# The running minimum of the scores: seeded from eviction to eviction, with ln 255 added on ScalarE

## What is computed

```python
q = _fq_sym(q, axis=-1)                       # rounded to 127 steps, per row
k = _fq_sym(k, axis=-1)
v = _fq_sym(v, axis=2)
attn = jnp.einsum('bhqd,bhkd->bhqk', q, k)    # 16 heads x 4096 queries x 8192 keys
attn = jax.nn.softmax(attn.astype(jnp.float32), axis=-1)
attn = _fq_unsigned(attn, axis=-1)            # round(255 * attn / max(attn)), per row
out = jnp.einsum('bhqk,bhkd->bhqd', attn, v)
```

## Time and profile before

| | us |
|---|---|
| runs shown | 6421.83, 7106.4, 6457.51 |
| their median | 6457.51 |
| the profiled execution | 6431.73 |
| its span, first to last instruction | 6430.2 |
| VectorE busy | 5619.6 (87%) |
| ScalarE busy | 4772.4 (74%) |
| GpSimd busy | 4588.0 (71%) |
| TensorE busy | 4487.4 (70%) |

### The profile page before, as it was taken

One profiled execution on the slowest core, in us unless ns is written; L12 is line 12 of the kernel. 1 busy time (PEld: TensorE's weight loads), 2 busy tenths in 40 slices (PEclk: granted clock), 3 DMA queues, 4 the chain that ended last, 5 costly groups with the idle time before them and its releaser, 6 DMA issues. The chain is left out here.

```text
span 6430.2 us, 141911 instructions
## 1 busy us (share of the span) xinstructions
PE 4487.4 (70%) x48939; PEld 2136.5 (33%) x49654; DVE 5619.6 (87%) x7587; ACT 4772.4 (74%) x6550; POOL 4588.0 (71%) x3259
## 2 busy tenths in 40 slices
PE   7556666666666666666666666666666646769999
PEld 3322222222222222222222222232222233455555
DVE  8799999999999999999999999999999936872222
ACT  5479998998999899989999988989989933331111
POOL 4578888888898888888888888888888823420000
PEclk9899999999999999999999999999999978979999
DMA  4267777777777777777777777777777730010000
GB/s 127 76 123 139 140 142 146 139 144 142 142 143 141 143 139 141 142 140 140 142 142 145 139 138 139 147 140 141 145 141 141 138 87 0 0 36 4 7 8 9
DMA packets 2231984, 735.80 MB, mean 114 GB/s; under 512 B 2175781, under 2 KB 2209416, under 8 KB 2225577
## 3 DMA queue, kind: packets, MB, share of 16 engines
q1 hardware_dynamic: 2196265, 576.08, 44.0%
q0 software_dynamic: 35456, 157.33, 13.8%
HBM read 168.97 MB, written 27.26 MB: 31 GB/s over the span
## 5 line engine op out<-in xcount | busy, mean ns | idle before, releaser
L914 DVE TENSOR_SCALAR_CACHE_REDUCE scores<-ring,step 128x2048 f32<-128x2048 f32 (+2 forms) x2560 | 4780.0, 1918 | 50.5 <-PE ring L841 38.1
L973 ACT ACTIVATE n_op<-scores,bias 128x2048 uint8<-128x2048 f32 x2048 | 4076.2, 1997 | 284.6 <-DVE m_rest L921 284.5
L789 POOL CAST nT<-pairs 128x2048 f16<-128x2048 uint8 x2048 | 3791.1, 1890 | 510.9 <-DMA pairs<-n_op 491.4
L841 PE MATMUL ring<-x_all,q_op 128*128 128x512 bf16 x7746 | 2147.6, 385 | 702.2 <-DVE scores L914 630.5
L841 PEld LDWEIGHTS ring<-x_all,q_op 128*128 128x128 bf16 x8192 | 682.2, 98 | 1854.1 <-DVE scores L914 1180.6
L838 PE MATMUL ring<-x_all,q_op 128*128 128x512 bf16 x1793 | 571.9, 389 | 775.2 <-DVE scores L914 744.1
L853 PE MATMUL pO<-nT,v_op 128*32 128x128 f16 x32768 | 659.0, 223 | 141.0 <-ACT att_g L991 109.0
L853 PEld LDWEIGHTS pO<-nT,v_op 128*32 128x32 f16 x32768 | 481.6, 98 | 590.2 <-issue 512.2
L838 PEld LDWEIGHTS ring<-x_all,q_op 128*128 128x128 bf16 x2048 | 116.7, 97 | 997.8 <-DVE scores L914 979.4
L973 ACT ACTIVATION_READ_ACCUMULATOR n_op<-scores,bias 128x1 f32 x2048 | 396.1, 193 | 0.0
L1752 DVE TENSOR_TENSOR h_up<-h_gate,pUp 128x512 f32<-128x512 f32 x112 | 76.9, 687 | 298.8 <-ACT h_gate L1741 298.8
(11 more groups left out here) (202 smaller groups left out, 3616.1 us busy)
## 6 DMA issues: line engine op xcount, KB each, us to landing
x_all<-keys_transposed POOLq DMA_DIRECT2D x128, 768.0 KB, 8.5
v_st<-value_integers POOLq DMA_DIRECT2D x128, 256.0 KB, 3.5
pairs<-n_op SPq DMA_TRANSPOSE x2048, 2.8
keys_transposed<-kT_s POOLq DMA_DIRECT2D x32, 384.0 KB, 3.3
cT<-in_ctx_T SPq DMA_DIRECT2D x32, 256.0 KB, 2.6
x_all<-in_x SPq DMA_DIRECT2D x2, 4096.0 KB, 16.2
q_op<-queries_transposed POOLq DMA_DIRECT2D x384, 16.0 KB, 8.4
value_integers<-v_int SPq DMA_DIRECT2D x1, 4096.0 KB, 13.0
```

What stands on the lines that cost most here:

```text
L789: nc.gpsimd.tensor_copy(nT[par][:, j * EK:(j + 1) * EK, :].rearrange("p (a c) b -> p a c b", c=2), src).then_inc(s_un, 1)
L841: mm = nc.tensor.matmul(slot(t, j)[:, n * BANK:(n + 1) * BANK], q_op[b][:, t * P:(t + 1) * P], k_op[b][:, at + n * BANK:at + (n + 1) * BAN ...
L914: nc.vector.tensor_scalar(score[t % 2][:, at:at + width * BANK], slot(t, j)[:, 0:width * BANK], step[b][:, t:t + 1], None, ALU.mult, ALU.m ...
L973: nc.scalar.activation(n_op[par][:, j * EW:(j + 1) * EW], score[par][:, j * EW:(j + 1) * EW], ACT.Exp, bias=bias[par][:], scale=-1.0, accu ...
```

## The change

The combination of minima (`make_bias`) and its place in VectorE's order go. From the second piece of a unit on, an eviction waits for the one in front of it and takes that one's minimum, column j - 1 of `m_part`, as a second per-row operand, so that column j holds the minimum over pieces 0 to j. ScalarE waits for the unit's last eviction, adds the constant ln 255 from a new tile to its column with an Identity activation of 128 x 1, and waits for that before the first exponential.

```diff
-        DVE_STEPS = "D0 BIAS D1 D2 D3 INV D4".split()
+        DVE_STEPS = "D0 D1 D2 D3 INV D4".split()
...
+        ln_255 = sb("ln_255", [P, 1], F32, xs)
...
+                nc.gpsimd.memset(ln_255[:], LN255).then_inc(s_init, 1)
...
                     dve.wait_ge(s_m, scored(u, j))
+                    least = None
+                    if j > 0:
+                        dve.wait_ge(s_mu, scored(u, j - 1))
+                        least = m_part[t % 2][:, j - 1:j]
                     nc.vector.tensor_scalar(score[t % 2][:, at:at + width * BANK], slot(t, j)[:, 0:width * BANK],
-                                            step[b][:, t:t + 1], None, ALU.mult, ALU.min,
+                                            step[b][:, t:t + 1], least, ALU.mult, ALU.min,
                                             accum_out=m_part[t % 2][:, j:j + 1]).then_inc(s_mu, 1)
-
-                def make_bias(u, par):
-
-                    dve.wait_ge(s_mu, scored(u, NM - 1))
-                    nc.vector.tensor_scalar(m_rest[par][:], m_part[par][:], LN255, None, ALU.add, ALU.min,
-                                            accum_out=bias[par][:]).then_inc(s_b, 1)
...
                     if j == 0:
+                        act.wait_ge(s_mu, scored(u, NM - 1))
+                        nc.scalar.activation(bias[par][:], m_part[par][:, NM - 1:NM], ACT.Identity,
+                                             bias=ln_255[:]).then_inc(s_b, 1)
                         act.wait_ge(s_b, u + 1)
...
+                act.wait_ge(s_init, 3)
```

More of the change, by code:

```diff
@@ L814, in _ @@
                 load_values(1, 1)
-                pool.wait_ge(s_init, 2)
+                pool.wait_ge(s_init, 3)
                 for b in range(2):
@@ L938, in period @@
                                 copy_scores(u + 1, int(x[1]), b, t1)
-                        elif x == "BIAS":
-                            make_bias(u, par)
                         elif t == 1 and exists(i - 1):
```

## The result

The changed kernel takes 6939.41 us (median of 4 runs, 6938.35 to 6943.46), where the kernel before has 6445.65 us (median of 3; a fourth run, 7106.4 us, fell in a slower state of the chip and is left out). The ratio is 1.0774, with a 95% interval of 1.0736 to 1.0812: slower, within the range of the forecast (6640 to 6990) and 53 us above its 6886. The profiled execution took 6939.89 us, so against the 6431.73 of before the loss is 508 us.

A forecast was written before the change was run, and what follows sets the result against it. VectorE, busy for 99% of the stage, was taken to bound the kernel. From the profiled 6431.73 us, + 389 (wait) + 123 (operand) - 41 (combination) - 17 (VectorE's waits for others) gave 6886 us, range 6640 to 6990.

The forecast's parts named there:

- the wait for the own engine: VectorE evictions from a unit's second piece on: waiting for the predecessor costs 0.19 us, 2048 times, + 389 us.
- the second operand: Same 2048 VectorE evictions: a further per-row operand costs 0.06 us each, + 123 us.
- the removed combination: VectorE, once per unit: dropping the combination of minima saves 0.08 us of starts, 512 times, - 41 us.
- VectorE's waits for others: VectorE's waits for TensorE and ScalarE, 35 us without the start's, were to halve: - 17 us.
- the two gaps of rows 5: Trace of `quantise`, end to waiting start: 0.03 us if the instruction carries the wait, 0.12 us if settled first.
- The rule weighed in the prediction: VectorE: eight copies with a semaphore behind each took as long as eight with one at the end.
- The two rows of 128 x 256: VectorE instructions in the earlier profile: 412 ns with two per-row operands, 293 ns with constants; 0.06 us for one.
- ScalarE's activation, nothing: ScalarE's added 128 x 1 activation per unit, 0.35 us, was taken to add nothing, covered by VectorE's longer unit.
- the free wait: Rival, VectorE evictions: waiting for the predecessor costs nothing; 6374 us, or 6497 with the operand's cost; chance 0.08.
- the short gap: Rival, VectorE evictions: each wait costs 0.11 us in all; 6599 us, or 6722 with the operand's cost; chance 0.12.
- the free operand: Rival, VectorE evictions: the wait costs, the further per-row operand doesn't; 6763 us; chance 0.17.
- that rival: TensorE's clock falls as its busy share drops and VectorE idles: 118 to 236 us more, 7004 to 7122; chance 0.12.

The follow-up runs named there:

- the carried wait: Changed kernel plus a semaphore increment nobody waits for, so the eviction itself carries the wait for its own engine: 6856.98 us, ratio 1.0635 to the kernel before.
- the first experiment: Kernel before plus 2048 waits of an eviction for the one in front, combination kept and no second operand: 6861.24 us, ratio 1.0642.
- the second: Kernel before plus a constant second per-row operand (3e38) in the same 2048 evictions, no wait added per eviction: 6549.69 us, ratio 1.0159.

## Why the prediction was right

The mechanism was the right one: the evictions lose their overlap and a fixed time behind it, and the operand comes on top. The start times of all evictions in the two traces give each term of its sum, in us. The first and the last eviction of the stage are 4823.5 us apart before and 5333.5 after, so 510 us are to be shared out.

| term | forecast | from the two traces |
|---|---|---|
| the wait for the own engine | + 389 | + 408 |
| the second operand | + 123 | + 134 |
| the removed combination | - 41 | - 40 |
| VectorE's waits for others | - 17 | + 8 |
| sum | + 454 | + 510 |

- *The wait for the own engine.* 0.205 us each, less what the reciprocal, which stands between two evictions once per head, hides of it; the forecast took 0.19. It was taken slightly under the 0.20 that L382 in the earlier trace rows gave; that row was the right one as it stood. Alone the waits cost 415 us, but that time has shorter and longer parts in it, as said there. That the order of the waits decides between the two gaps of rows 5 is shown by the carried wait, which moved the gap behind the read's end from 0.12 to 0.04 us. The rule weighed in the prediction, of "VectorE: DVE Perf Modes", section "The DRAIN you can't avoid", in the Trainium skill, would have made this zero; 415 us speak against it for an instruction whose successor otherwise starts before it ends.
- *The second operand.* 0.06 us each as forecast, between 0.061 us (alone) and 0.065 us (in the changed kernel). The two rows of 128 x 256 gave the right size.
- *The removed combination.* Before, the next eviction starts 0.078 us behind it all through the stage. The run that took it away without seeds brought a new wait that hid this gain.
- *VectorE's waits for others.* This is the step that failed, if a small one. They did not halve. In the views of the waits they are 38.1 + 8.6 = 46.7 us before and 46.7 + 9.5 = 56.2 after.
- *ScalarE's activation, nothing.* Right for the change, but the reason given does not carry it. It was argued from the mean slack, which alone did not cover the activation (47 us); that a longer unit of VectorE is the cover, as the prediction also says, was not separated from the bias that comes an eviction earlier, which it counted as mere slack.

So the waits for others were 25 us off, the wait for the own engine 19 and the operand 11, nearly all of the 54 us by which + 454 fell short of the profiled 508. The unit was forecast at 10.2 to 10.3 us and is 10.30.

Of the rivals, the free wait and the short gap are excluded by the first experiment, the free operand by the second. TensorE's clock did fall, from 0.99 to 0.97 in the stage, as that rival said it might, but VectorE hardly felt it: its late starts behind the lower clock are 30 us before and 24 us after, and the median with more matmuls is 8 us lower, not the 118 to 236 that were priced. The reason named against it in the prediction, that a slower VectorE leaves TensorE more time per slot, fits the two runs with more matmuls: they gain 8 us at the changed kernel's pace, which the intervals don't tell from nothing, and 134 us with the carried wait, where a unit is shorter.

No version here beats the kernel before. The 41 us on offer would need the combination to go without a wait for the eviction just in front, without a later bias, and without a further operand in the evictions.

## What to carry to other kernels

On an engine that sets the pace, a value that passes from one instruction to the very next costs the overlap of the two and the way through the semaphore, here 0.20 us each time, even if it saves an instruction of 0.08 us. Independent work between writer and reader hides that time only as far as it lasts: an eviction of 1.7 us hid all of it, the combination, worth 0.08 us of starts, hid 0.08 us. And where an engine's mean slack is to cover something, look for the one place per round where another engine waits for it: mean slack isn't slack there.

## What the runs showed of the hardware

- Which instruction carries a wait matters: 0.12 us from the end of the read to the next start when the wait is settled in an event-semaphore instruction ahead, 0.04 us when the eviction carries it. The instruction ahead itself starts 0.04 us behind the end of the read, and the eviction 0.08 us behind that.
- The time runs from the writer, not from the instruction in front: with the combination in between (the wait alone) or the reciprocal (the changed kernel), the waiting eviction also starts 0.21 us behind the writer's read.
- A second per-row operand on VectorE costs 0.06 us, in duration and from start to start, also where the instructions overlap.
- With the carried wait, two matmuls per unit whose product is not used made the kernel faster by 134 us, as the granted clock rose from 0.94 to 1.00; in the kernel before, at 0.99, the same two did nothing (ratio 0.9993). Why the clock was lowest in the kernel with the carried wait, and lower than in the slower changed kernel (0.97), is open.
- A GpSimd instruction on 128 x 1 with two per-row operands took 0.37 us and 0.20 us more to the next one that waits for it.
